# The first feed-forward batch prepared inside the last attention batch, in one program block

## The chip, the cores and the metric

The kernel runs on one core of one Trainium2 chip. The metric is the device time of one execution in microseconds (us); lower is better. A core has a matrix engine (TensorE, PE in the profile; its weight loads are listed as PEld), VectorE (DVE), ScalarE (ACT), GpSimd (POOL) and SyncE (SP), which here only issues DMAs. Each engine runs its own instructions in order, and they meet only at semaphores.

## The reference, cut to what matters

```python
x = L0_attn_x                                   # (8, 1024, 512)
mod = (_silu(L0_c) @ L0_wmod).reshape(8, 6, 1, 512)
sa, ca, ga, sb, cb, gb = mod[:, 0], ..., mod[:, 5]      # ga, gb: |gate| at least 0.25
h = _layernorm(x) * (1 + ca) + sa
x = x + ga * attn(h)         # 16 heads of 32; q, k, v = (h @ W + b) reshaped (b, h, dh, t);
                             # softmax over k.v * temperature, applied to q
h = _layernorm(x) * (1 + cb) + sb
x = x + gb * ffn(h)
# ffn: scores = h @ w_router; per batch the 512 of 1024 tokens with the highest scores are kept
#   processed = gelu(selected @ W1 + b1) @ W2 + b2       W1 (512, 2048), W2 (2048, 512)
#   output = hidden, plus sigmoid(score) * processed at the kept tokens
```

There are 8 batches of 1024 tokens.

## The kernel before, in words

There are two functions, each with its own SBUF and PSUM buffers and its own program block, one after the other: `attention_phase` and `ffn_phase`. At the end of a block all engines meet before the next one starts.

**Attention.** A loop over 8 batches holds 4 groups each, 32 groups in all. A group handles 256 tokens, as 16 pairs `p` of two units; a unit is one 128x1024 tile of scores. For a unit PE writes the scores into one of three PSUM slots (L408), DVE takes the row maximum (`row_max`, L702), ACT takes the exponential into `probs` (`exp_unit`, L595), which frees the slot, and PE multiplies the probabilities of an earlier pair with q (`products`, L455). Between these, PE makes k, v and q of the next group (L418, L430) and transposes its normalised rows (L441); ACT copies them out of PSUM (L568, L585, L575); POOL normalises, adds biases and splits values into two half-precision parts; DVE takes layernorm statistics (L660 of x, L745 of the new x) and divides q by the sums (L758, L763). POOL also finishes the group before: `residual` (L904), `normed_before`, `h_times`, `h_plus`, `base_times` and `base_plus` (L859 to L937), after which SP stores the rows `h_rows` and `out` (L344, L345); DVE makes the router scores (`dot_router`, L731). SP copies k and v into the stacks of the next group (L337).

**Rank.** Behind the loop SP writes the scores of all batches to memory, 4 bytes at a time (`store_scores`, L377), and loads those of batch 0 into every partition (`srow`, L382). For each of 8 tiles of tokens DVE counts the scores above (L77) and the equal ones that come earlier (L82), both over 1024 scores; `find_slots` turns the rank into a slot number (L90 to L97).

**Feed-forward.** All eight batches run the same body: a loop of 3 times two batches, then two batches written out. At the start SP loads W1 and W2 as eight pieces of 1 MB into four staging buffers (L1079); ACT makes the high part of each (`high_part`, L1157), DVE the low part (`low_part`, L1201). POOL stores number and weight of the kept tokens into `sel_rows` (`store_kept`, L104: 8 indirect DMAs); SP loads them as `kept` (L1064), DVE makes integers of them (`numbers`, L1206), POOL gathers rows of h into `hs` (L1276) and of the base into `bs` (L1279), PE transposes `hs` (L1106), and ACT and DVE make its two halves `fT` (L1162, L1211). Then for each of 16 slices `f`: `ff1` (12 matmuls, L1116), gelu on ACT (L1177), two splits on DVE (L1224, L1226) and `ff2` of the slice before (12 matmuls, L1129). Within the slices of one batch DVE also ranks the next one (one tile of tokens in each of slices 0 to 7, slots in slice 7, `numbers` in slice 10), and PE transposes its rows in slices 12 to 15. At the end DVE adds the bias (L1247), and POOL scales, adds the base and stores (L1294 to L1306).

## Time and profile before

| | us |
|---|---|
| median of 3 runs | 2504.0 |
| lowest and highest | 2500.78 and 2508.22 |
| profiled execution | 2516.56 |
| its span | 2514.8 |

| engine | busy us | share of the span |
|---|---|---|
| PE | 2284.4 | 91% |
| PEld | 899.7 | 36% |
| DVE | 1972.2 | 78% |
| ACT | 1483.7 | 59% |
| POOL | 1412.4 | 56% |

The span is the time between the first and the last record of the trace; 1.8 us lie around it. A busy share is a mean over stages: attention takes about two thirds of the span, the feed-forward part most of the rest, and each of them has to be read by itself, as does the stretch between them.

### The profile page before, as it was taken

Reading aid. Unit: us, or ns where it says so; the run is one execution under the profiler, and the core shown is the slowest. Engines: PE = TensorE matmul, PEld = TensorE weight load, DVE = VectorE, ACT = ScalarE, POOL = GpSimd, SP = SyncE. Lnnn points to the kernel's source line nnn. Section 1 sums busy time; section 2 is a strip of 40 time slices with the busy share of each in tenths; the row PEclk is TensorE's granted clock in tenths of the full one; section 3 lists DMA queues with packets and bytes.
Section 4 is the critical chain, followed back from the end, with each engine's and each line's share of the span. In section 5 each row is a group of like instructions: output and inputs, shape, how many; then the busy total and the mean of one; then the engine's idle time right before and its main releaser. Section 6 shows DMA issues by size and latency. Waiting matters only on the chain. (4 is left out here: it accounts for less than half of the span.)

```text
span 2514.8 us, 42424 instructions
## 1 busy us (share of the span) xinstructions
PE 2284.4 (91%) x12884; PEld 899.7 (36%) x12884; DVE 1972.2 (78%) x2698; ACT 1483.7 (59%) x2631; POOL 1412.4 (56%) x1233
## 2 busy tenths in 40 slices
PE   7999999999999999999999999950499999999996
PEld 2333333333333333333333333320244444444443
DVE  5899999999999999999999999953546645754632
ACT  1788888888888888888878888840311111111110
POOL 4566666676667666766666666660225444452531
PEclk9999999999999999999999999985699999999998
DMA  6233242333232333232233233373411112021110
GB/s 205 64 90 81 70 100 70 82 81 86 69 94 69 86 85 76 73 98 73 72 76 95 75 75 90 75 60 60 149 43 35 49 42 63 21 58 46 38 39 17
DMA packets 125227, 184.40 MB, mean 73 GB/s; under 512 B 43776, under 2 KB 43776, under 8 KB 124936
## 3 DMA queue, kind: packets, MB, share of 16 engines
q1 hardware_dynamic: 115216, 155.97, 25.9%
q0 software_dynamic: 9728, 25.23, 3.2%
q8 instruction: 108, 1.77, 0.3%
q14 instruction: 175, 1.43, 0.2%
HBM read 68.74 MB, written 43.16 MB: 44 GB/s over the span
## 5 line engine op out<-in xcount | busy, mean ns | idle before, releaser
L595 ACT ACTIVATE probs<-sc,nmax 128x1024 f32<-128x1024 f32 x1024 | 1137.2, 1116 | 249.7 <-DVE nmax L702 237.0
L702 DVE TENSOR_REDUCE nmax<-sc 128x1 f32<-128x1024 f32 x1024 | 1212.3, 1214 | 61.6 <-PE sc L408 55.8
L408 PE MATMUL sc<-stacks 128*128 128x512 f16 x2048 | 617.8, 383 | 51.8 <-ACT probs L595 36.5
L455 PE MATMUL acc<-probs,qn 128*32 128x512 f32 x4136 | 552.3, 606 | 2.1 <-DVE qn L763 1.2
L1177 ACT ACTIVATE g<-ff,b_col 128x512 f32<-128x512 f32 x128 | 88.0, 687 | 578.3 <-PE ff L1116 536.9
L1129 PE MATMUL ff<-w,g 128*128 128x512 f16 x1536 | 352.4, 379 | 14.7 <-DVE g L1226 13.9
L408 PEld LDWEIGHTS sc<-stacks 128*128 128x128 f16 x2048 | 154.6, 98 | 579.8 <-ACT probs L595 327.5
L1116 PE MATMUL ff<-fT,w 128*128 128x512 f16 x1536 | 353.9, 381 | 1.6 <-DVE fT L1211 1.6
L1224 DVE CAST g<-g 128x512 f16<-128x512 f32 x128 | 76.9, 600 | 290.8 <-ACT g L1177 243.5
L1129 PEld LDWEIGHTS ff<-w,g 128*128 128x128 f16 x1536 | 148.8, 98 | 199.2 <-DVE g L1226 21.5
L1116 PEld LDWEIGHTS ff<-fT,w 128*128 128x128 f16 x1536 | 151.0, 98 | 180.3 <-issue 5.7
L418 PE MATMUL pj<-wk,hT 128*128 128x512 f16 x792 | 205.8, 384 | 0.0
L595 ACT ACTIVATION_READ_ACCUMULATOR probs<-sc,nmax 128x1 f32 x1024 | 205.4, 201 | 0.0
L418 PE MATMUL pj<-wv,hT 128*128 128x512 f16 x792 | 202.6, 379 | 0.0
L430 PE MATMUL pj<-hT,wq 128*128 128x256 f16 x1584 | 194.2, 273 | 0.9 <-ACT qT L585 0.9
L430 PEld LDWEIGHTS pj<-hT,wq 128*128 128x128 f16 x1584 | 154.8, 98 | 46.5 <-ACT qT L585 1.2
L104 POOL DMA_INDIRECT sel_rows<-tok,slot x64 | 68.8, 1076 | 181.2 <-DVE slot L95 163.5
L913 POOL TENSOR_TENSOR hbuf<-hbuf,rows 128x1024 f32<-128x1024 f32 x66 | 155.8, 2361 | 17.8 <-DVE qn L763 17.6
L455 PEld LDWEIGHTS acc<-probs,qn 128*32 128x32 f32 x4136 | 81.6, 108 | 222.8 <-issue 217.2
L1294 POOL TENSOR_TENSOR y<-y,gb_row 128x512 f32<-128x512 f32 x32 | 46.6, 1461 | 192.0 <-DVE y L1247 192.0
L880 POOL TENSOR_TENSOR kv<-kv,k_bias 128x512 f32<-128x512 f32 x66 | 84.1, 1274 | 91.2 <-ACT kv L568 54.3
L880 POOL TENSOR_TENSOR kv<-kv,v_bias 128x512 f32<-128x512 f32 x66 | 84.5, 1281 | 87.0 <-ACT kv L568 87.0
(123 smaller groups left out, 2302.9 us busy)
## 6 DMA issues: line engine op xcount, KB each, us to landing
stacks<-k SPq DMA_DIRECT2D x528, 64.0 KB, 2.0
stacks<-v SPq DMA_DIRECT2D x528, 64.0 KB, 2.0
xt<-in_L_attn_x SPq DMA_DIRECT2D x140, 128.0 KB, 2.6
h_rows<-hbuf SPq DMA_DIRECT2D x132, 128.0 KB, 2.2
out<-base SPq DMA_DIRECT2D x132, 128.0 KB, 2.5
rows<-mod_rows SPq DMA_DIRECT2D x32, 256.0 KB, 4.0
stage<-in_L_ffn_W SPq DMA_DIRECT2D x8, 1024.0 KB, 9.9
probs<-in_L_wmod SPq DMA_DIRECT2D x4, 1024.0 KB, 10.7
```

The source lines that it names most:

```text
L408: mm = nc.tensor.matmul(slot(g, v)[:, half * D:(half + 1) * D], stacks[g % 2][:, 0, hq, i * P:(i + 1) * P], stacks[g % 2][:, 1, hq, half * ...
L418: mm = nc.tensor.matmul(pj[:], hT16[par][:, a, cc, p * P:(p + 1) * P], w[:, z, cc, :], start=(t == 0), stop=(t == len(terms) - 1))
L430: mm = nc.tensor.matmul(pj[:, ci * 2 * P:(ci + 1) * 2 * P], wq16[:, z, cc, co * P:(co + 1) * P], hT16[par][:, a, cc, :], start=(t == 0), s ...
L455: mm = nc.tensor.matmul(acc[at:at + DH, :], qn[:, (p // 2) % 2, p % 2, h2, :], probs[:, (2 * p + h2) % PROBS, half * D:(half + 1) * D], st ...
L595: nc.scalar.activation(probs[:, u % PROBS, :], slot(g, ring_at(p, h2)), ACT.Exp, bias=nmax[:, u % PROBS:u % PROBS + 1], accum_out=rsum[:, ...
L702: nc.vector.tensor_reduce(nmax[:, u % PROBS:u % PROBS + 1], slot(g, ring_at(p, h2)), AX.X, ALU.max, negate=True).then_inc(max_done, 1)
L880: nc.gpsimd.tensor_tensor(kv32[kk % 2][:], kv32[kk % 2][:], row, ALU.add).then_inc(kv_bias, 1)
L913: nc.gpsimd.tensor_tensor(dst, a, rows[:, row:row + 1, :].broadcast_to([P, SUBS, D]), op).then_inc(s_hm, 1)
L1116: mm = nc.tensor.matmul(ff[f % 2][:], w1_16[:, z, cc, f * P:(f + 1) * P], fT16[:, par, a, cc, :], start=(t == 0), stop=(t == len(terms) - 1))
L1129: mm = nc.tensor.matmul(acc[kt][:], g16[:, f % 2, a, kt * P:(kt + 1) * P], w2_16[:, z, f, :], start=(f == 0 and t == 0), stop=(f == FC - 1 ...
L1177: nc.scalar.activation(g32[:, f % 2, :], ff[f % 2][:], ACT.Gelu_apprx_tanh, bias=b1_col[:, f:f + 1], scale=1.0 / WS).then_inc(gelu_done, 1)
L1224: nc.vector.tensor_copy(g16[:, f % 2, 0, :], g32[:, f % 2, :]).then_inc(g_hi, 1)
```

## The change

Both phases become one function, `block_phases`, with one program block. Large buffers are shared: `room1` holds the attention weights and both `hT16`, and later W1; `room2` holds the even stacks, `k16`, `v16`, `hT32` and `kv32`, and later W2; `room3` holds `xhat` and three of the four `xt`, and later two staging buffers (four before). The feed-forward accumulators take the three PSUM slots, `acc` and `pj`.

- The attention loop runs 7 times, and the last batch is written out (`body(LAST, True)`). The feed-forward part has its first two batches written out, a loop of 2 times two, and two written out.
- `store_scores` moves into every attention batch, behind the row stores of group 1, for the batch before. `b1_col` (2048 biases, 4 bytes each) is loaded at the start of the kernel, ahead of the temperatures.
- `count_above` compares with "at least" for earlier tiles and "above" for the rest, together 1024 scores, and looks for equals over 128 only. `find_slots` has one more small addition.
- In the last batch DVE ranks batch 0 within groups 0 to 2 (`rank_first`), and POOL stores the kept numbers at the end of group 2 and gathers `hs` in group 3. The last group makes no k, v and q for a next one; the last two make no transposes, and the last three load no x and take no statistics of it. In group 3 SP loads weight pieces 0 to 2, ACT and DVE split pieces 0 (and ACT 1 and 2), and PE, ACT and DVE transpose and split the kept rows of batch 0.
- The other weight pieces (order W1, W2, W1, W2, ...) are loaded and split in slices of the first feed-forward batch (`first`), as are the statistics of the last group's x, its router scores, the scores and weights of batch 7 and the rank of batch 1, whose slots come in slice 8 and whose `numbers` come in slice 11.

```diff
-    nc.vector.tensor_scalar(r.cmp_out[:, 0], r.srow[:], r.s8[:, t:t + 1], 0.0, ALU.is_gt, ALU.add,
+    own = t * P
+        nc.vector.tensor_scalar(r.cmp_out[:, 0:own], r.srow[:, 0:own], r.s8[:, t:t + 1], 0.0, ALU.is_ge, ALU.add,
+                                accum_out=r.before[:, t:t + 1]).then_inc(r.s_cmp, 1)
+    nc.vector.tensor_scalar(r.cmp_out[:, own:T], r.srow[:, own:T], r.s8[:, t:t + 1], 0.0, ALU.is_gt, ALU.add,
...
# SP, attention body
+                    if last and g == 0:
+                        sp.wait_ge(s_sc, 16 * (B - 1))
+                        load_scores(0)
+                    if last and g == GB - 1:
+                        load_kept(0, 0)
+                        sp.wait_ge(t_pe, NG)
+                        load_weights(0)
                     sp.wait_ge(x2_done, b * GB + g + 1)
-                    load_x((g + 3) % 4, ahead[g])
-                    replicate((g + 1) % 2, 0, b * GB * 4 + 4 * (g + 1) + 2)
+                    if not (last and g >= GB - 3):
+                        load_x((g + 3) % 4, ahead[g])
+                    if last and g == GB - 1:
+                        load_weights(1)
+                        load_weights(2)
+                    else:
+                        replicate((g + 1) % 2, 0, b * GB * 4 + 4 * (g + 1) + 2)
...
+                    if g == 1:
+                        store_scores(batch_before)
...
# SP, behind the attention batches
+            load_weights(3)
+            sp.wait_ge(pv_done, ALL_PAIRS)
+            sp.dma_start(b2_row, b2.partition_broadcast(P)).then_inc(s_b, 16)
+            sp.wait_ge(r.s_slot, 1)
+            sp.wait_ge(s_sc, 16 * B)
+            load_scores(1)
+            sp.wait_ge(post_done, NG + 1)
+            store_rows(NG - 1, (NG - 1) % 2)
+            for j in range(4, 6):
+                load_weights(j)
+            sp.wait_ge(s_dot, 2 * NG + 2)
+            store_scores(B - 1)
+            for j in range(6, 8):
+                load_weights(j)
...
# ACT, last group, then the first feed-forward batch
+                        if end and p == 3:
...
+                            high_part(0)
+                        if end and p == 8:
+                            high_part(1)
+                        if end and p == 12:
+                            high_part(2)
+                        if end and p > NQ and p % 2 == 1:
+                            kept_high(0, 0, (p - NQ) // 2, aux[0])
...
+                    if first and f == 0:
+                        high_part(3)
+                    if first and f == 2:
+                        high_part(4)
+                    if first and f == 4:
+                        high_part(5)
...
# DVE, last batch, then the first feed-forward batch
+                if g == 0 and p == 7:
...
+                    count_above(nc, dve, r, 0, only)
+                if g == 0 and p == 14:
+                    count_above(nc, dve, r, 1, only)
...
+                if g == 2 and p == 8:
+                    dve.wait_ge(s_tok, 3)
+                    find_slots(nc, dve, r, r.tokens[:, 0:TB, :], only)
...
+                        if end and p == 1:
+                            numbers(0, 0)
+                        if end and p == 7:
+                            low_part(0)
+                        if end and p > NQ and p % 2 == 1:
+                            kept_low(0, 0, (p - NQ) // 2, aux[0])
...
+            q_over_sums(B, -1, PAIRS // 2 - 1)
+            low_part(1)
+            gated(B, -1, 1)
...
+                        if f == 0:
+                            low_part(2)
+                        if f == 1:
+                            for s in range(SUBS):
+                                stats_of_x2(B, 0, s)
+                            aggregate2(B, 0)
+                        if f == 2:
+                            low_part(3)
+                        if f == 3:
+                            count_tile(0)
+                            low_part(4)
...
+                        if f == 8:
+                            count_tile(6)
+                            count_tile(7)
+                            slots_of_next()
...
+                        if f == 11:
+                            numbers(nb, npar)
...
# POOL, last batch
+                    if last and g == GB - 2:
+                        wait_alone(r.s_slot, 1)
+                        store_kept(nc, r, sel_rows, range(0, TB // 2))
                     behind_qn(b, g, 7)
                     base_plus(b, g)
+                    if last and g == GB - 2:
+                        store_kept(nc, r, sel_rows, range(TB // 2, TB))
```

## Rows read from the trace of the kernel before

**Rows 1.** The page: busy tenths of PE in 40 slices of the span.

```profile
PE   7999999999999999999999999950499999999996
```

**Rows 2.** Windows by stage: length, then busy us (instructions) per engine, granted clock, DMA.

```profile
1568.50:1619.00 50.50, 49.35 (x307) 18.26 (x309) 48.68 (x64) 43.58 (x80) 34.25 (x30) 1.00 0.30 75
...
1672.50:1787.00 114.50, 0.00 (x0) 0.00 (x0) 38.54 (x62) 14.37 (x10) 37.08 (x27) 0.52 0.73 107
...
1805.90:1885.00 79.10, 79.10 (x376) 36.93 (x375) 39.07 (x72) 12.37 (x19) 15.47 (x16) 1.00 0.13 34
```

**Rows 3.** Timeline, the hand-over: start us, length us, engine, line, operation.

```profile
1668.61 1.12 ACT L595 ACTIVATE probs<-sc,nmax 128x1024 f32<-128x1024 f32 x1
...
1670.41 1.92 PE L455 MATMUL acc<-probs,qn 128*32 128x512 f32 x16 [1.21 <-DVE qn L763]
...
1674.30 11.50 SPq L377 DMA_DIRECT2D score_rows<-scores  x6
...
1676.99 0.25 DVE L750 BATCH_NORM_AGGREGATE mv<-stats 128x2 f32<-128x6 f32 x2 [0.15 <-DVE stats L745]
...
1687.82 2.34 POOL L937 TENSOR_TENSOR base<-base,x 128x1024 f32<-128x1024 f32 x1
1712.30 0.37 SPq L382 DMA_DIRECT2D srow<-score_rows  x1
```

**Rows 4.** Timeline, first weight pieces and first feed-forward matmuls.

```profile
1752.89 2.40 SPq L1079 DMA_DIRECT2D stage<-in_L_ffn_W  x4
...
1758.12 1.91 ACT L1157 ACTIVATE w<-stage 128x2048 f16<-128x2048 f32 x1 [3.33 <-DMA stage<-in_L_ffn_W]
...
1762.38 4.42 SPq L1079 DMA_DIRECT2D stage<-in_L_ffn_W  x1
...
1798.10 8.15 PE L1116 MATMUL ff<-fT,w 128*128 128x512 f16 x24 [1.60 <-DVE fT L1211]
```

**Rows 5.** Groups of instructions by shape, 1468 to 1670 us (four groups): busy us, mean ns.

```profile
L702 DVE TENSOR_REDUCE nmax<-sc 128x1 f32<-128x1024 f32 x129 | 152.8, 1215 | 6.5 <-PE sc L408 5.7 <-issue 0.2
...
L660 DVE BATCH_NORM_STATS2 stats<-xt 128x6 f32<-128x512 f32 x8 | 5.5, 682 | 0.0
...
L418 PE MATMUL pj<-wv,hT 128*128 128x512 f16 x96 | 24.6, 379 | 0.0
...
L430 PE MATMUL pj<-hT,wq 128*128 128x256 f16 x195 | 24.1, 273 | 0.0
```

**Rows 6.** Timeline, rank of the last batch up to the transposes of its rows.

```profile
2364.00 1.27 DVE L77 TENSOR_SCALAR_CACHE_REDUCE cmp_out<-srow,s 128x1024 bf16<-128x1024 f32 x1
...
2365.20 1.28 DVE L82 SCALAR_TENSOR_TENSOR cmp_out<-srow,s,earlier 128x1024 bf16<-128x1024 f32 x1
...
2367.01 0.22 DVE L95 SCALAR_TENSOR_TENSOR slot<-rank,first,drop 128x8 int32<-128x8 f32 x1
...
2377.16 0.98 POOL L104 DMA_INDIRECT sel_rows<-tok,slot  x1 [0.30 <-issue]
...
2381.24 0.17 DVE L1206 CAST kept_i<-kept 128x4 int32<-128x4 f32 x1 [1.12 <-DMA kept<-sel_rows]
...
2390.85 0.65 PE L1106 MATMUL aux<-id,hs 128*128 128x128 f32 x4 [0.25 <-DMA hs<-h_rows,kept_i]
```

**Rows 7.** Timeline, start of a feed-forward batch: a split beside POOL's work.

```profile
2338.00 1.48 DVE L1224 CAST g<-g 128x512 f16<-128x512 f32 x1
```

**Rows 8.** Waits of PE, 1798 to 2500 us: total us, times, longest.

```profile
PE ff L1129 <- DVE g L1226: 13.9, 13, 1.5
```

**Rows 9.** Timeline, start of the attention: two matmuls of scores at the low clock.

```profile
70.75 1.03 PE L408 MATMUL sc<-stacks 128*128 128x512 f16 x2 [2.20 <-DMA stacks<-v]
```

**Rows 10.** DMA issues by line: count, KB each, median us to landing.

```profile
score_rows<-scores SPq DMA_DIRECT2D x8, 4.0 KB, 21.1
...
b_col<-in_L_ffn_b SPq DMA_DIRECT2D x1, 8.0 KB, 10.7
```

**Rows 11.** Timeline of POOL in the group from 1568.5 us: `base_times`.

```profile
1613.12 2.80 POOL L913 TENSOR_TENSOR base<-hbuf,rows 128x1024 f32<-128x1024 f32 x1
```

More of the change, by code:

```diff
@@ L286, in attention_phase, with batches, n_of, only @@
         assert GB * RING % SLOTS == 0 and GB * UNITS % PROBS == 0
+        ALL_PAIRS = NG * PAIRS + LAG
+        ALL_FREED = SLOTS + NG * RING
+        LAST = B - 1
+        def batches(eng, body):
+            for par in range(2):
+                body(0, par, par == 0, False, False)
+            with eng.Fori(1, B // 2 - 1) as bb:
+                for par in range(2):
+                    body(bb, par, False, False, False)
+            for par in range(2):
+                body(B // 2 - 1, par, False, par == 1, True)
+        def n_of(bb, par, per, off):
+            return bb * (2 * per) + (per * par + off)
+        def only(per, off):
+            return off
         def mod_bank(j):
@@ L514, in _ @@
                     nxt = (g + 1) % 2
+                    end = last and g == GB - 1
                     for p in range(PAIRS):
@@ L546, in _ @@
                             whole(piece)
-                        if 2 * p + 2 == T_AT:
+                        if 2 * p + 2 == T_AT and not (last and g >= GB - 2):
                             pe.wait_ge(s_xhat, b * GB + g + 3)
@@ new lines, in low_part @@
+            def low_part(j):
+                k = j // 2
+                dve.wait_ge(w_hi, j + 1)
+                if j % 2 == 0:
+                    hi, lo = (w1_16[:, z, :, k * D:(k + 1) * D] for z in range(2))
+                else:
+                    hi, lo = (w2_16[:, z, 4 * k:4 * (k + 1), :] for z in range(2))
+                nc.vector.scalar_tensor_tensor(out=lo, in0=stage[:, j % 2], scalar=WS, in1=hi, op0=ALU.mult,
+                                               op1=ALU.subtract).then_inc(w_lo, 1)
@@ L773, in _, with body @@
+            def body(b, last):
                 for g in range(GB):
+                    load = not (last and g >= GB - 3)
+                    end = last and g == GB - 1
                     for p in range(PAIRS):
@@ L786, in _ @@
                             aggregate2(b, g)
[L787 removed]
+                        if (p == 9 or p == 11) and load:
                             if p == 9:
@@ L809, in _ @@
-            dve.wait_ge(r.s_const, 2)
-            nc.vector.tensor_copy(r.tokens[:, :, 0], r.tok_i[:]).then_inc(s_tok, 1)
-            nc.vector.memset(r.first[:], 0.0)
-            nc.vector.tensor_copy(r.s8[:], scores[:, 2:2 + TB])
-            weights(slice(0, (B - 1) * TB), 1)
-            dve.wait_ge(s_tok, 3)
-            dve.wait_ge(r.s_srow, 16)
-            for t in range(TB):
-                count_above(nc, dve, r, t, lambda per, off: off)
-            find_slots(nc, dve, r, r.tokens[:, 0:TB, :], lambda per, off: off)
@@ L825, in _ @@
+            batches(dve, ffn)
         @block.gpsimd
@@ L961, in _ @@
                     behind_qn(b, g, 4)
-                    split_kv(nxt, 2, n4 + 3)
+                    if not end:
+                        split_kv(nxt, 2, n4 + 3)
                     h_times(b, g)
```

740 lines of the change are left out of this document (389 added, 351 removed).

## The prediction, as it was made before the changed kernel ran

> **What bounds the kernel now.** I began with the busy slices of PE [rows 1]: PE is full in attention and in the feed-forward part, and two or three slices between them stand nearly empty. The windows [rows 2] put sizes to it. A group of attention lasts 50.5 us with PE busy 49.35 and DVE 48.68: both are full there, ACT (43.6) and POOL (34.3) are not. From 1672.5 to 1787 PE does nothing. So work moved into the last attention batch meets a full DVE; it isn't free because PE gets lighter.
>
> The hand-over, read in the timeline [rows 3, 4]: the last exponential ends at 1669.73 (call it E), PE's last products at 1672.33, and the first `ff1` starts at 1798.10. That is 125.8 us without useful matmuls. In order: seven score stores (1674.3 to 1712.3, 5.4 us each), sixteen counts and the slots (1716.7 to 1737), the last row stores and the meeting of the engines (to 1752.9), kept numbers, gather, weights, transposes (to 1798). Then the first 24 matmuls take 8.15 us, where later a matmul takes 0.216 (79.1 us for 376, transposes among them, [rows 2]) and 24 some 5.18.
>
> **The change, part by part.** Sum against the profiled execution, 2516.6 us; the median of the runs is 2504.0, 0.5% lower, and I apply the difference to it.
>
> *1. The gap.* `ff1` of batch 0 needs the split rows, the first weight piece and a free PSUM slot, all ready by E or soon after; PE's last products end at E + 2.6 and `ff1` can follow. Saved: **125.8 us**, less what follows.
>
> *2. DVE in the last batch.* A pass over 1024 scores starts 1.20 us after the one before (2364.00 to 2365.20, [rows 6]). With 0.13 us of it fixed (an estimate; the 8-element slot step is 0.22 long, same group) three passes over 1024 + 128 elements are 1.6 us, against 2.4 before. Eight tiles are 12.7; the slots 1.0, scores and weights 0.9, `numbers` 0.2, one `low_part` 2.2, four `kept_low` 2.4: 19.4. Gone are three groups' statistics of x, 6 x 0.68 [rows 5] and aggregation, 4.8. Net 14.6. In four groups DVE waits 6.5 us for PE [rows 5] and about 2 for others. If all of that slack takes up work, 6 us stay; if none, 14.6. PE is as full as DVE in groups 0 to 2, so a burst of DVE isn't made good later there; in group 3 PE loses 12.3 of k and v and 6 of q (half of 24.6, a quarter of 24.1, [rows 5]) and DVE is the only bound. I take **+10.5**.
>
> *3. ACT in the last group.* It loses k, v, q and transposed copies and gains three `high_part` of 1.91 [rows 4] and four copies of 0.6, some 45 us of work in 52. But each 1.91 delays a slot, and the three slots give DVE about 1 us of room (estimated from its spacing of 1.5 us per unit): 3 x 1. **+3** (0 to 6).
>
> *4. A new wait in group 3.* DVE does `numbers` behind pair 1 of group 3, and the rest of its row maxima is queued behind it, so all engines wait with it. POOL reaches `base_times` 44.6 us into a group [rows 11], here about 3 earlier since it splits no hT and 2 later with the longer group: 43.5. Then 2.4, four indirect stores of 1.29, `base_plus` 2.4, four more stores: 58.7; from there `numbers` came 3.1 us behind the last store's end (2378.14 to 2381.24, [rows 6]): 62. DVE gets there at 52.5 + 6.8 = 59.3. **+3** (0 to 8). POOL's gather (4 x 1.27) ends ahead of its `residual`. SP's first weight piece, queued behind the kept numbers, needs 5.2 us from issue to ACT (1752.89 to 1758.12, [rows 4]) and comes to ACT at pair 3 just in time.
>
> *5. The start.* The b1 load of 2048 single elements now stands ahead of the temperatures, Wq and further modulation weights, while the DMA engines are full. The nearest rows: it landed after 10.7 us [rows 10], SP's next load then took 4.4 us to issue (at 1762.38, [rows 4]), and a store of 1024 such elements took 5.4. **+4** (0 to 10). The same kind of store in each attention batch comes at the start of group 2, some 20 us before the next copies of k: nothing, unless it takes longer than it did. The Trainium skill (DMA: Bandwidth & Descriptors, Specifications) puts the least transfer for full rate at 512 bytes; the rate of 4 KB in 5.4 us agrees, and a reader may leave the page out.
>
> *6. The first feed-forward batch.* Here a chain speaks against the change. S = E + 2.6 is the start of `ff1` 0, a slice's 12 matmuls are 2.59 us. ACT's `high_part(3)` behind gelu 0 waits for a piece that SP may load only after `low_part(1)` (S + 0.4): landed S + 6, done S + 8, gelu 1 done S + 8.7, its split S + 9.9, then the statistics of the last group: S + 11.5. Only now can POOL normalise that group: statistics to `base_plus` took 12.9 us (1677.24 to 1690.16, [rows 3]), S + 24.4. SP waits for just that, issues 8 row stores (4 us), then weight piece 4: S + 28.9, landed about 8 us later among 2 MB of other transfers (5.2 to 10): S + 37. ACT stands at `high_part(4)` behind gelu 2 since S + 11.3, with gelu 3 queued behind it. So split 3 ends at S + 40.9, and PE, done with `ff1` 4 at S + 20.7, waits for it: **+20.2** (14 to 25). In such a wait PE's clock falls: after the hand-over 24 matmuls took 8.15 for 5.18 [rows 4] and the granted clock of the empty stretch was 0.52 [rows 2], near the lower of its two levels, 1.2 GHz: **+3**.
> The second wait: the slots of batch 1 come in slice 8, not 7. By DVE's queue from S + 40.9 (counts, low parts, router scores between splits) they are ready at S + 70.6. From slots to landed rows took 23.6 us (2367.2 to 2390.8, [rows 6]): S + 94.2. PE reaches the transposes behind `ff2` 11 at S + 87.7: **+6.5** (3 to 10). Behind 94.2 come four transposes of 0.44, three `ff1` and four `ff2`, 19.9: it ends at S + 114.1. Before, the first batch took 87.4 (1798.1 to 1885.5; PE full to 1885, [rows 2]). Difference **+26.7**, the 3 us of clock being in both.
>
> *7. The other seven batches.* At their start DVE's splits run beside POOL's work and take 1.48 us for 0.43 [rows 7], and PE waits for them 13.9 us in all [rows 8], some 2.2 in each of six batches that also count. Counts 0.8 shorter let the second and third split end earlier: about 1.4 a batch, **-8** (-11 to 0).
>
> Sum: -125.8 + 10.5 + 3 + 3 + 4 + 26.7 - 8 = **-86.6**; 2516.6 becomes 2430, and on the median 2504 - 87 = **2417 us**.
>
> **The rivals.**
> *A, the covers hold.* DVE's slack takes the rank, `numbers` doesn't wait, weight piece 4 lands at S + 34 and the transposes wait 3: 6 + 1 + 0 + 1 + 20 - 10 on -125.8 is -108: 2396. For it: DVE has 8 us of waits in four groups. Against: the wait for piece 4 is in the program's order and doesn't hang on a price.
> *B, the inserts cost their full time.* 14.6 + 6 + 7 + 8 + 33 - 3 = +65.6 on -125.8 is -60: 2444. For it: PE and DVE take turns with three slots, and a burst on one is felt by the other.
> *C, PE goes to its low clock in group 3*, since it is busy only 32 of 52 us there. At 1.2 GHz two score matmuls take 1.03 [rows 9] for 0.61, eight products twice 1.06: 32 x 1.03 + 16 x 2.1 + 4 is 70, and the group lasts 15 to 18 us longer: 2433. Against: its gaps would be about a microsecond, and with such gaps in attention the granted clock was 1.00 [rows 2]. The Trainium skill (TensorE: Matmul & The Clock Gate, Part 1: The HAM clock gate) has half rate as the state of an idle engine that activity lifts; by it C is possible, and the clock after the empty stretch agrees (0.52).
> *D, slower than before.* The score stores within the loop hold up the copies of k and v in the DMA queues. The place is SP's queue at the start of group 2; the next copies come 22 us into the group. The gain of 87 is spent when each of seven batches loses 12.4 us, so from some 34 us per store on. It took 5.4 in a row of seven [rows 3], though a landing of 21.1 us stands as the median, queued behind each other [rows 10]. At 36 us per store: 2519.
> *E, the hand-over isn't emptied.* The chain slots, stores, kept numbers, gather isn't done when the transposes of group 3 are due, and a serial stretch returns. It would have to slip by some 20 us before PE waits; were it late by 105, 2500.
>
> **How the numbers follow.** Forecast 2417, its own range 2405 to 2430 (parts 4 to 7 within half their bounds): 0.50. A 0.20, B 0.20, C 0.05, D 0.02, E 0.03. A range of 2388 to 2450 takes in the forecast, C and nearly all of A and B and leaves out D, E and the tails, under 2 in 10. 0.3% is 7.5 us, about what this measurement can tell from no change: faster 0.95 (forecast, A, B, C), same 0.03 (E), slower 0.02 (D).
>
> **What would show it.** Part 1: no PE gap over some 5 us between the last products and `ff1`. Parts 2 to 4: the last batch takes 218 us instead of 202, with a DVE wait at `numbers` of about 3. Part 5: the first scores at 75 instead of 70.8. Part 6: ACT waits for stage piece 4 for some 25 us in slice 2, PE some 20 behind `ff1` 4, then some 6 for the gathered rows. Part 7: six batches of about 86 us instead of 87.5. I would be wrong if PE runs through slices 2 to 4 without a gap, if the loop's groups leave 50.5 us, or if group 3 shows a clock under 0.9.

## The result and the profile after

| | before | after |
|---|---|---|
| median, us | 2504.06 | 2433.23 |
| lowest and highest of 4 runs | 2500.78 and 2508.22 | 2431.43 and 2438.28 |
| profiled execution | 2516.56 | 2431.43 |
| its span | 2514.8 | 2429.7 |

The ratio of the times is 0.9715, with a 95% interval from 0.9704 to 0.9727: 71 us faster. The forecast was 2417, 87 us faster, with a range of 2388 to 2450.

The page of the changed kernel: busy tenths of PE and its granted clock, in 40 slices of the span.

```profile
PE   7999999999999999999999999877689999999996
PEclk9999999999999999999999999999899999999998
```

The slices 5, 0 and 4 of [rows 1] are gone. In their place stand five dented ones: the last attention batch (8, 7, 7) and the first feed-forward batch (6, 8).

The end of attention in the timeline of the changed kernel (start us, length us, engine, line, operation): last exponential, last products, first `ff1`.

```profile
1687.88 1.11 ACT L804 ACTIVATE probs<-sc,nmax 128x1024 f32<-128x1024 f32 x1
...
1689.68 1.92 PE L599 MATMUL acc<-probs,qn 128*32 128x512 f32 x16 [2.33 <-DVE qn L1037]
...
1691.53 0.39 PE L728 MATMUL sc<-qT,room 128*128 128x512 f16 x1
```

`ff1` begins as the last products end. The 125.8 us of [rows 3, 4] have become nothing.

What was given back shows in the waits of all engines of the changed kernel, 1680 to 1850 us (total us, times, longest).

```profile
ACT room L825 <- DMA room<-in_L_ffn_W: 32.9, 3, 28.4
...
PE sc L741 <- DVE probs L1165: 22.5, 1, 22.5
...
PE pj L659 <- DMA stacks<-h_rows,kept_i: 8.6, 1, 8.6
```

And in SP's own queue, changed kernel: row stores of the last group, then weight pieces 4 and 5.

```profile
1718.35 0.34 SPq L436 DMA_DIRECT2D h_rows<-hbuf  x1
...
1721.80 0.43 SPq L437 DMA_DIRECT2D out<-base  x1
1722.27 1.38 SPq L472 DMA_DIRECT2D room<-in_L_ffn_W  x2
```

SP issues piece 4 at 1722.27, right behind the eight stores. ScalarE stood for it until 1731.2, the splits behind it came late, and PE stood 22.5 us. That is the chain of step 6 of the forecast.

For the last attention batch I cut both traces at the start of the last exponential of each group. Columns: length, then busy us (instructions) of PE, PEld, DVE, ACT and POOL, granted clock, DMA share, GB/s. First a further profiled execution of the kernel before (2503.05 us, near its median), then the changed kernel.

```profile
1465.20:1516.30 51.10, 49.45 (x306) 17.95 (x306) 47.54 (x65) 42.46 (x77) 32.89 (x29) 1.00 0.32 80
1516.30:1565.30 49.00, 48.03 (x300) 17.71 (x296) 47.30 (x65) 42.09 (x78) 32.87 (x29) 1.00 0.36 94
...
1614.40:1663.60 49.20, 48.22 (x306) 17.76 (x302) 47.31 (x64) 42.12 (x78) 32.90 (x29) 1.00 0.31 77
```

```profile
1461.30:1514.50 53.20, 49.27 (x302) 17.58 (x298) 51.52 (x76) 42.31 (x77) 32.87 (x29) 1.00 0.37 91
1514.50:1571.40 56.90, 49.98 (x297) 16.84 (x296) 55.10 (x85) 42.18 (x79) 32.44 (x29) 1.00 0.31 75
1571.40:1627.10 55.70, 48.88 (x283) 16.42 (x286) 51.89 (x75) 40.93 (x74) 29.39 (x26) 0.97 0.21 47
1627.10:1687.90 60.80, 41.40 (x222) 9.10 (x214) 50.37 (x64) 44.23 (x73) 26.06 (x19) 0.92 0.30 89
```

In group 1 DVE is 7.8 us busier (55.10 for 47.30) and the group 7.9 us longer, with DVE 97% busy both times: no slack took up work there. Group 0 did hide some (4.0 us more work, 2.1 us more time), group 2 (before: DVE busy 47.30 of 49.10) the reverse (4.6 and 6.6). Together the three have 16.4 us more work and take 16.6 us longer. Group 3 is 11.6 us longer though DVE has only 3 us more to do: there something waits.

How far can one group of one trace be trusted? Group 1 has the same code in the changed kernel and in nine of those built on it below. It lasts 56.9 us in six of these ten and 58.1 or 58.2 in four. Group 2 has the same code in nine and lasts 54.0 to 57.9. So a difference of a microsecond in group 1, or of one to four in group 2, needs no cause in an edit. Group 3, with all its inserts and the wait in place, stays within 60.8 to 61.6 in the changed kernel and in the four below that leave it as it is.

Where the time went, stage by stage, against both profiled executions of the kernel before. The stages are cut at the starts of the last exponential of an attention batch, of the first `ff1` and of the writes of y.

| stage | before, 2516.56 | before, 2503.05 | after | difference to each |
|---|---|---|---|---|
| start and seven attention batches | 1469.5 | 1465.2 | 1461.3 | -8.2, -3.9 |
| last attention batch | 199.1 | 198.4 | 226.6 | +27.5, +28.2 |
| last exponential to first `ff1` | 129.5 | 122.9 | 3.6 | -125.9, -119.3 |
| first feed-forward batch | 87.6 | 86.2 | 121.1 | +33.4, +34.8 |
| other batches, to the last y | 609.1 | 608.6 | 597.2 | -11.9, -11.4 |
| to the end of the span | 19.9 | 19.9 | 19.9 | 0, 0 |
| sum | 2514.8 | 2501.3 | 2429.7 | -85.1, -71.6 |

The profiled execution that the forecast was made on was 12.5 us above its median, and 6.6 us of that lay in the hand-over, which the change takes out whole. Against it the change looks worth 85 us; against a typical one, 72. The difference in the first line is not shown to be the change's. Start and seven batches take 1463.4 to 1469.5 us in three traces of the old program (the third has only the cheaper count, below) and 1461.3 to 1465.1 in eleven of the new one, and these ranges overlap.

### The profile page after: what moved, and what is told of

It reads as the page before. It is cut to its first block, busy times and chain, and to the rows that moved or that the text cites. A ratio compares the mean times of both kernels' runs of the same rounds, so it can differ in the third digit from the quotient of the medians.

```text
span 2429.7 us, 41301 instructions
## 1 busy us (share of the span) xinstructions
PE 2272.0 (94%) x12772; PEld 886.5 (36%) x12772; DVE 1903.2 (78%) x2806; ACT 1477.5 (61%) x2616; POOL 1367.7 (56%) x1205
## 4 chain that ended last, share of the span: by engine, by line
PE 65%; DVE 16%; issue 9%; POOL 4%; ACT 3%; DMA 1%; SPq 1%; DVEq 0%; POOLq 0%; ACTq 0%
PE sc L552 13%; PE sc L741 13%; PE acc L599 13%; PE sc L728 12%; DVE nmax L976 9%; PE pj L562 8%; PE pj L574 5%; POOL x L1314 3%; DVE qn L1037 2%; ACT probs L804 2%; DVE stats L1019 1%; PE sc L585 1%; PE sc L614 1%; DVE rinv L1032 0%; DMA room<-in_L_ffn_W 0%
## 5 line engine op out<-in xcount | busy, mean ns | idle before, releaser
L562 PE MATMUL pj<-room 128*128 128x512 f16 x1536 | 395.3, 381 | 0.4 <-ACT qT L794 0.4
L741 PE MATMUL sc<-room,probs 128*128 128x512 f16 x1536 | 354.7, 381 | 26.8 <-DVE probs L1165 26.8
L552 PE MATMUL sc<-room 128*128 128x512 f16 x1024 | 309.4, 384 | 40.7 <-ACT probs L804 24.1
L552 PE MATMUL sc<-stacks 128*128 128x512 f16 x1024 | 309.6, 384 | 38.3 <-ACT probs L804 37.7
L741 PEld LDWEIGHTS sc<-room,probs 128*128 128x128 f16 x1536 | 150.3, 98 | 209.8 <-DVE probs L1165 27.6
L562 PEld LDWEIGHTS pj<-room 128*128 128x128 f16 x1536 | 150.1, 98 | 188.4 <-issue 8.9
L574 PE MATMUL pj<-room 128*128 128x256 f16 x1536 | 188.3, 273 | 1.1 <-ACT qT L794 0.9
L728 PE MATMUL sc<-stacks,room 128*128 128x512 f16 x768 | 175.6, 379 | 0.0
L574 PEld LDWEIGHTS pj<-room 128*128 128x128 f16 x1536 | 150.0, 98 | 45.5 <-ACT qT L794 1.8
L728 PE MATMUL sc<-qT,room 128*128 128x512 f16 x512 | 163.4, 382 | 1.1 <-issue 1.1
L1294 POOL TENSOR_TENSOR room<-room 128x512 f16<-128x512 f32 x128 | 149.0, 1164 | 10.6
```

What stands on the lines that cost most here:

```text
L552: mm = nc.tensor.matmul(slot(g, v)[:, half * D:(half + 1) * D], stacks[g % 2][:, 0, hq, i * P:(i + 1) * P], stacks[g % 2][:, 1, hq, half * ...
L562: mm = nc.tensor.matmul(pj[:], hT16[par][:, a, cc, p * P:(p + 1) * P], w[:, z, cc, :], start=(t == 0), stop=(t == len(terms) - 1))
L574: mm = nc.tensor.matmul(pj[:, ci * 2 * P:(ci + 1) * 2 * P], wq16[:, z, cc, co * P:(co + 1) * P], hT16[par][:, a, cc, :], start=(t == 0), s ...
L728: mm = nc.tensor.matmul(ff[f % 2], w1_16[:, z, cc, f * P:(f + 1) * P], fT16[par][a][:, cc, :], start=(t == 0), stop=(t == len(terms) - 1))
L741: mm = nc.tensor.matmul(ff2[kt], g16[:, f % 2, a, kt * P:(kt + 1) * P], w2_16[:, z, f, :], start=(f == 0 and t == 0), stop=(f == FC - 1 an ...
L1294: nc.gpsimd.tensor_tensor(dst[:, 1], kv32[kk % 2][:], dst[:, 0], ALU.subtract).then_inc(kv_split, 1)
```

## The experiments

The theory at this point: PE's wait for weight piece 4 and the late gathered rows are two waits in series in the first feed-forward batch; in the last attention batch DVE's added work counts in full; group 3 has a further loss in SP's chain. The rival for each: some other engine or DMA traffic holds the same time, so that the wait moves and doesn't go.

A ratio is to runs of the kernel before taken beside each experiment, whose medians lie between 2504.8 and 2509.1 us. So differences between two kernels are better read from the ratios (0.001 is 2.5 us) than from the times.

**The kernel before, once more.** It gave the second column of the table.

> The kernel before, profiled once more, to see what of the 85 us between the two profiled executions belongs to the change. Theory 1 (the profiled execution of before was a long one, 12.5 us above its median, and the surplus lies in the start and in the attention loop): the empty stretch of PE between last products and first ff1 is again 125 to 127 us, and the first scores start earlier than 70.8 us or the loop's seventh batch is reached earlier than 1400.9 us. Theory 2 (the surplus lies in the hand-over itself, in the 4-byte stores): the empty stretch is 113 to 118 us, and start and loop are as in the first profile.

Measured: 2503.05 us. From last products to first `ff1` 119.2 us, with 4.8 us for each store of the scores where [rows 3] has 5.4.

**Weight pieces 4 and 5 ahead of the last row stores.**

```diff
+            for j in range(4, 6):
+                load_weights(j)
             sp.wait_ge(post_done, NG + 1)
             store_rows(NG - 1, (NG - 1) % 2)
-            for j in range(4, 6):
-                load_weights(j)
```

> The changed kernel with SP's loads of weight pieces 4 and 5 ahead of its wait for the last base_plus and of the last row stores. Theory: the wait of ACT for piece 4 (28.4 us) and PE's wait of 22.5 us behind it go away, and so does the low clock behind it (about 2.6 us); the wait for gathered rows (8.6 us) stays within 2 us. 24 to 26 us faster than the changed kernel, some 2408 us. Rival (the empty time is only handed on: the piece still lands late among row stores and gather, or another wait, for the router scores or the base, takes its place): 0 to 12 us faster, with a PE wait of over 10 us elsewhere in the first feed-forward batch.

Measured: 2419.17 us, ratio to the kernel before 0.9647 (0.963 to 0.9665): 14 us less than the changed kernel by the times and 17 by the ratios, not 24 to 26. The waits of PE in this kernel, 1690 to 1800 us:

```profile
PE pj L659 <- DMA stacks<-h_rows,kept_i: 9.4, 1, 9.4
PE sc L741 <- DVE probs L1165: 3.5, 2, 2.8
```

The wait for piece 4 is gone but for 3.5 us, so its cause is shown. From first `ff1` to first y it takes 103.2 us for 121.1: 17.8 us less in the stage that was changed. In attention, which was not, this profiled execution is 5.2 us longer. The second wait stayed, and part of the gain went to DVE, whose splits now run beside POOL's work for the last group (timeline of DVE, same kernel):

```profile
1714.91 2.20 DVE L1163 CAST probs<-probs 128x512 f16<-128x512 f32 x1 [1.83 <-ACT probs L878]
1717.15 2.72 DVE L1165 TENSOR_TENSOR probs<-probs 128x512 f16<-128x512 f32 x1
1719.79 2.32 DVE L1153 COPY s<-scores 128x8 f32<-128x8 f32 x1
```

With POOL idle these take 0.43, 0.69 and 0.17 us (the copy in the changed kernel, at 1734.81). In the changed kernel most of this work of POOL fell into the time in which DVE stood still anyway. The Trainium skill (GPSIMD Engine Reference, Specifications) says that GpSimd's SBUF interfaces are shared with VectorE, with contention for some kinds of VectorE instructions. That these three are slow beside POOL and fast without it agrees.

**The biases loaded last at the start.** The load of `b1_col` moves behind all other first loads.

```diff
-                sp.dma_start(b1_col[:], b1.rearrange("(f p) -> p f", p=P)).then_inc(s_b, 16)
...
             load_x(2, 2)
+            with nc.allow_non_contiguous_dma(reason="2048 biases, once"):
+                sp.dma_start(b1_col[:], b1.rearrange("(f p) -> p f", p=P)).then_inc(s_b, 16)
```

> The changed kernel with the load of b1 (2048 single elements) behind the last loads of the start, not ahead of the temperatures. Prediction's part 5: 4 us faster (0 to 10), the first scores start 3 to 5 us earlier than 67.0 us. Rival (the start isn't held by that load, as the profile of after suggests with first scores at 67.0 against 70.8): within 1 us of the changed kernel.

Measured: 2434.23 us, ratio 0.9707 (0.9691 to 0.9724): not to be told from the changed kernel, though the intervals leave room for some 3 us. The first scores start at 68.5 us here, 67.0 in the changed kernel, 68.8 and 70.8 in the two of before. With the load moved they come later and not earlier, so it does not hold up the start.

**The rank of batch 0 done twice**, with the second results unused.

```diff
                     count_above(nc, dve, r, 0, only)
+                    again(0)
```

> The changed kernel with each of the eight counts of batch 0 in the last attention batch done twice (23 more passes on DVE, 12.7 us of work, plus their waits). Theory (DVE bounds the last attention batch and its slack is used up): 11 to 15 us slower than the changed kernel. Rival (a good part is covered by waits of DVE for PE and ACT): 4 to 9 us slower. If it is over 16, the inserts cost more than their length, by disturbing the turn of PE, DVE and ACT.

Measured: 2451.35 us, ratio 0.9774 (0.9755 to 0.9792): 18 us above the changed kernel by the times, 15 by the ratios, for 12.7 us of added passes. The groups of the last attention batch:

```profile
1464.40:1522.30 57.90, 50.42 (x302) 18.72 (x298) 54.93 (x86) 42.60 (x77) 32.88 (x29) 0.96 0.38 90
1522.30:1586.80 64.50, 53.53 (x298) 18.17 (x296) 60.94 (x109) 42.28 (x79) 32.49 (x29) 0.93 0.28 67
```

The columns are those of the windows above. The groups are 4.7 and 7.6 us longer than in the changed kernel, 14.7 in all four. DVE is busy 12.7 us more in them. So work on DVE costs here about its length, or a little more. In the two groups above PE's clock is lower, 0.96 and 0.93 where the changed kernel has 1.00; whether that is the surplus was not shown.

**The slots of batch 1 in slice 7** (built on the kernel with pieces 4 and 5 early): DVE's list of the first feed-forward batch is put in another order.

```diff
+                            count_tile(0)
                         if f == 2:
...
-                        if f == 8:
+                        if f == 6:
+                            low_part(4)
                             count_tile(6)
+                        if f == 7:
                             count_tile(7)
                             slots_of_next()
+                            low_part(5)
+                        if f == 8:
+                            weights(slice(LAST * TB, B * TB), 2)
```

> The kernel with weight pieces 4 and 5 loaded early (e1), and in the first feed-forward batch VectorE ranks batch 1 earlier: tile 0 behind the statistics in slice 1, tiles 1 and 2 in slice 3, 3 in slice 4, 4 and 5 in slice 5, 6 in slice 6, 7 and the slots in slice 7; low parts 4, 5 move to slices 6 and 7. My theory: the 9.4 us that PE waits for the gathered rows in e1 is the chain slots, stores, kept numbers, gather (20 us from slots at 1752.2 to landed rows), so 6 us earlier slots take 6 to 9 us off: 2410 to 2413 against 2419. Rival: the DMA side (weight pieces 6 and 7, 4-byte numbers) sets when the rows land, and the wait moves by less than 2 us: 2418 to 2421. Second rival: counts beside POOL's work in slice 3 cost three times their length and delay the splits that PE waits for, giving the gain back: 2417 to 2422.

Measured: 2408.42 us, ratio 0.9611 (0.9595 to 0.9627): 11 us less than without it by the times, 9 by the ratios. The waits of PE, 1690 to 1800 us:

```profile
PE sc L741 <- DVE probs L1165: 5.2, 3, 4.3
PE pj L659 <- DMA stacks<-h_rows,kept_i: 2.9, 1, 2.9
```

The wait for the gathered rows fell from 9.4 to 2.9 us, so it was the chain from DVE's rank. The wait for DVE's splits grew from 3.5 to 5.2: a small part of what the second rival said. From first `ff1` to first y it takes 96.9 us for 103.2. That is what the new order gave, 6.4 us, the 4.8 of the two waits and some clock: without the new order PE ran at 0.50 for six microseconds behind the longer wait. Nearly all the rest of the gain in these two traces (5.4 us) lies ahead of the first `ff1`, where nothing was changed.

**POOL's stores of the kept numbers earlier in group 2.**

```diff
+                    if last and g == GB - 2:
+                        wait_alone(r.s_slot, 1)
+                        store_kept(nc, r, sel_rows, range(0, TB // 2))
                     behind_qn(b, g, 6)
...
                     base_times(b, g)
                     if last and g == GB - 2:
-                        wait_alone(r.s_slot, 1)
-                        store_kept(nc, r, sel_rows, range(0, TB // 2))
+                        store_kept(nc, r, sel_rows, range(TB // 2, TB))
                     behind_qn(b, g, 7)
                     base_plus(b, g)
-                    if last and g == GB - 2:
-                        store_kept(nc, r, sel_rows, range(TB // 2, TB))
```

The first four stores stand one step earlier, behind the last split of v.

> e4, and in group 2 of the last attention batch POOL stores the kept numbers ahead of its work on the base rows instead of around it (first four behind the last split of v, four behind the product with the gate). My theory: the wait of VectorE at the integer kept numbers in group 3 (4.5 us in the changed kernel) goes, and the whole group with it: 4 us less than e4. Rival: VectorE's wait only stands in for one that comes anyway (ScalarE and PE have their own work to catch up with, or POOL's late rows delay the next group), and the time stays within 1.5 us of e4.

Measured: 2412.16 us, ratio 0.9632 (0.9606 to 0.9659): no gain. SP's queue shows why:

```profile
1637.62 0.33 SPq L436 DMA_DIRECT2D h_rows<-hbuf  x1
...
1642.01 0.43 SPq L437 DMA_DIRECT2D out<-base  x1
1642.48 0.43 SPq L461 DMA_DIRECT2D kept<-sel_rows  x1
```

SP loads the kept numbers only behind the row stores of group 2, and those wait for `base_plus`, which now came behind all eight stores of POOL. DVE waited 5.2 us at `numbers` instead of 4.5. I had moved the work on POOL and left out the queue of SP between it and DVE.

**The inserts of group 3 made tiny** (changed kernel).

```diff
-                            high_part(0)
+                            high_part(0, True)
...
-                            low_part(0)
+                            low_part(0, True)
...
+                if few:
+                    dst, src = dst[:, 0:1, 0:2], src[:, 0:1, 0:2]
```

> The changed kernel, in which the high parts of weight pieces 0, 1 and 2 and the low part of piece 0 take 2 columns in the last attention group instead of 2048 (so most of W1's first piece, the high half of W2's first and W1's second piece are left out, and the output with them); waits and loads stay. It measures what these four inserts cost group 3: 3 x 1.9 us on ScalarE, 2.3 us on VectorE. My forecast had +3 for ScalarE's and 2.2 of VectorE's time: about 5 us less than the changed kernel, 2428. Rival (the inserts cost their full length and push PE to its low clock): 8 to 14 us less, 2419 to 2425, and the granted clock of the group's second half above 0.9 where it was 0.65 to 0.91. Second rival: nothing, VectorE's other work bounds the group.

Measured: 2431.12 us, ratio 0.9698 (0.9682 to 0.9714), 2 us less than the changed kernel by the times, 4 by the ratios, and not clearly to be told from it. Its last group lasted 56.3 us for 60.8, 4.5 less:

```profile
1516.40:1574.60 58.20, 51.44 (x297) 16.93 (x296) 55.22 (x85) 42.30 (x79) 32.45 (x29) 0.97 0.31 75
1574.60:1631.20 56.60, 51.28 (x283) 16.76 (x286) 51.99 (x75) 40.84 (x74) 29.17 (x26) 0.91 0.21 46
1631.20:1687.50 56.30, 41.45 (x222) 9.24 (x214) 48.06 (x64) 39.63 (x73) 24.25 (x19) 0.91 0.34 97
```

But groups 1 and 2, in which nothing was changed, lasted 2.2 us longer, with a clock of 0.97 and 0.91. That is within the spread of these groups. The 4.5 us of group 3 are not, so the four inserts cost about that, near the 5.2 of steps 2 and 3 together. The wait at `numbers` stands in this group too, 4.9 us long.

**Only the cheaper count**, in the kernel before: two blocks and the hand-over stay as they were.

```diff
-    nc.vector.tensor_scalar(r.cmp_out[:, 0], r.srow[:], r.s8[:, t:t + 1], 0.0, ALU.is_gt, ALU.add,
...
+        nc.vector.tensor_scalar(r.cmp_out[:, 0, 0:own], r.srow[:, 0:own], r.s8[:, t:t + 1], 0.0, ALU.is_ge, ALU.add,
+                                accum_out=r.before[:, t:t + 1]).then_inc(r.s_cmp, 1)
+    nc.vector.tensor_scalar(r.cmp_out[:, 0, own:T], r.srow[:, own:T], r.s8[:, t:t + 1], 0.0, ALU.is_gt, ALU.add,
...
```

> The kernel before (two program blocks, rank between them) with only the new count_above and find_slots: 1152 scores per tile in three passes instead of 2048 in two. My theory: seven feed-forward batches that rank the next one become about 2 us shorter each, as in the changed kernel (85.5 for 87.5), and the rank in the hand-over by 8 x 0.8 = 6 us: 2504 - 20 = 2484 (2482 to 2490). Rival from my forecast: 1.4 us per batch, so 2504 - 10 - 6 = 2488. Second rival: the shorter batches come from something else in the new program (PSUM places, buffers), and only the 6 us of the hand-over show: 2498.

Measured: 2484.33 us, ratio 0.9919 (0.99 to 0.9938): 20 us faster, as the first theory said. The writes of y in this kernel, and PE's waits from 1866 us on:

```profile
1866.46 2.48 DVE L1258 SCALAR_TENSOR_TENSOR y<-ff,b_row 128x512 f32<-128x512 f32 x4 [1.27 <-PE ff L1140]
1951.96 2.48 DVE L1258 SCALAR_TENSOR_TENSOR y<-ff,b_row 128x512 f32<-128x512 f32 x4 [1.27 <-PE ff L1140]
```

```profile
PE ff L1140 <- DVE g L1237: 5.0, 7, 0.8
```

A batch takes 85.5 us, as in the changed kernel, for 87.5 before, and PE's waits for splits are 5.0 us for 13.9 [rows 8]. So the small edit in `count_above` alone is worth 20 us in the old program. From the first to the last y it saves 11.8 us (596.8 for 608.6), nearly all of the 11.9 or 11.4 that these batches gained in the changed kernel; most of the rest lies in the hand-over.

**`numbers` behind pair 3, and the high parts late.** Three kernels on top of the one with the slots in slice 7: the integer kept numbers behind pair 3 instead of 1; high parts of pieces 1 and 2 behind the last exponential and gelu 0; both.

```diff
-                        if end and p == 1:
+                        if end and p == 3:
                             numbers(0, 0)
```

```diff
-                        if end and p == 8:
-                            high_part(1)
-                        if end and p == 12:
-                            high_part(2)
...
+            high_part(1)
             act.wait_ge(s_d, 1)
...
                     if first and f == 0:
+                        high_part(2)
+                    if first and f == 1:
                         high_part(3)
```

> e4 (weight pieces 4 and 5 early, slots of batch 1 in slice 7), and VectorE makes the integer kept numbers behind pair 3 of the last attention group instead of pair 1. The kept numbers land in the box's row order at 1639.7 us of e4, where VectorE stands since 1635.2; POOL's gather starts only behind the division of pair 4, at 1643.6. My theory: the wait of 4.5 us goes from the group and nothing takes its place, since VectorE bounds it: 2408 becomes 2403 to 2405, group 3 lasts 56 to 57 us for 60.8. Rival (as in e5, which gained nothing): the group is held by ScalarE's inserts and three slots, and the time stays at 2407 to 2410. Second rival: the gather comes later and PE waits for the rows at pair 8 of the group: slower than e4 by 2 to 5 us.

> e4, and ScalarE makes the high parts of weight pieces 1 and 2 behind the last exponential and behind gelu 0 instead of within the last attention group (high part 3 follows behind gelu 1). If ScalarE's inserts delay VectorE by the slots they hold back, as the shrunk inserts showed (group 3 lasted 56.3 us for 60.8 with all four inserts gone), two of them moved out give back 2 to 3 us in the group, and cost nothing behind it, where ScalarE waits for PE: 2405 to 2406. Rival: half of that saving was VectorE's low part alone, and the moved parts delay the low parts of pieces 1 and 2 and with them PE in slice 1 or 4: 2408 to 2411.

> Both changes of the two runs beside it. If both theories hold they add up: 4.5 + 2.5 us under e4, 2400 to 2403, since one is a wait of VectorE early in the group and the other a wait for slots in its middle. If one of them fails, the time is that of the other alone; if the wait at the numbers had covered part of what ScalarE catches up with, the sum is smaller than the parts by about 2 us.

Measured: 2412.58 us, ratio 0.9627 (0.961 to 0.9644); 2409.13 us, ratio 0.9618 (0.9598 to 0.9638); 2409.58 us, ratio 0.9614 (0.9596 to 0.9631). None can be told from the kernel they build on (0.9611), so the 2403 to 2405 of the first, the 2405 to 2406 of the second and the 2400 to 2403 of both together did not come. With the high parts late the last group did shrink, to 57.4 us for 60.8, with a wait at `numbers` of 4.8 still in it:

```profile
1630.60:1688.00 57.40, 40.17 (x213) 8.48 (x212) 49.02 (x64) 41.03 (x70) 25.08 (x19) 0.91 0.32 93
```

With `numbers` at pair 3 alone it didn't shrink (60.4). The kernel with both shows what took the place of the wait, first DVE's wait in its last group, then ScalarE's:

```profile
DVE rinv L1031 <- ACT probs L804: 3.8, 1, 3.8
```

```profile
ACT room L825 <- DMA room<-in_L_ffn_W: 3.6, 1, 3.6
```

DVE no longer waits for the kept numbers, but ScalarE now stands at the high part of piece 0, and DVE behind it. SP issues that piece behind the kept numbers, for which it waits until POOL's last store has landed. The wait at `numbers` had covered this one.

**Piece 0 ahead of the kept numbers**, on top of both.

```diff
-                        load_kept(0, 0)
                         sp.wait_ge(t_pe, NG)
                         load_weights(0)
+                        load_kept(0, 0)
```

> The kernel with both changes of the run before (kept numbers made behind pair 3, high parts of pieces 1 and 2 late), and SP loads weight piece 0 ahead of the kept numbers instead of behind them. There the wait at the numbers was gone but ScalarE stood 3.6 us at the high part of piece 0 in pair 3, because SP issues that load only behind the kept numbers, for which it waits 4.7 us until POOL's last store has landed; VectorE then stood 3.8 us for ScalarE. My theory: these two waits are one chain in SP's queue, and without it group 3 lasts about 54 us for 57.9: ratio to the kernel before 0.9600 (0.959 to 0.961) for 0.9614, that is 2404 to 2407 where the kernel before takes 2504 to 2507. Rival: a third wait takes their place (PE at its low clock, or the kept numbers landing later behind the megabyte of weights, so that VectorE stands at pair 3 again): group 3 stays at 57 to 58 us and the ratio at 0.961 to 0.963.

Measured: 2402.91 us (2399.93 to 2406.73), ratio 0.9592 (0.9577 to 0.9607). This is the lowest ratio of all and as expected (0.959 to 0.961), but its interval overlaps that of its base. ScalarE's and DVE's waits in the last group are now small. First ScalarE, then DVE:

```profile
ACT room L825 <- DMA room<-in_L_ffn_W: 1.1, 1, 1.1
```

```profile
DVE kept_i L1067 <- DMA kept<-sel_rows: 0.7, 1, 0.7
...
DVE rinv L1031 <- ACT probs L804: 0.5, 1, 0.5
```

So these two waits did come from SP's order. But the theory also said that group 3 would last 54 us, and its rival that it would stay at 57 to 58. Groups 2 and 3, first of the kernel with both changes, then of this one:

```profile
1575.50:1632.20 56.70, 49.94 (x289) 16.57 (x288) 52.34 (x75) 40.86 (x73) 30.48 (x26) 0.97 0.22 48
1632.20:1690.10 57.90, 40.56 (x212) 9.16 (x212) 49.06 (x64) 41.12 (x70) 25.07 (x19) 0.88 0.31 92
```

```profile
1572.30:1626.30 54.00, 48.50 (x283) 16.57 (x286) 51.85 (x75) 40.73 (x73) 29.09 (x26) 0.97 0.22 48
1626.30:1683.90 57.60, 42.38 (x222) 9.11 (x214) 50.54 (x64) 41.20 (x70) 26.40 (x19) 0.88 0.33 95
```

Group 3 went from 57.9 to 57.6 us, as the rival said. DVE waits less there, but the same 64 instructions keep it busy 1.5 us longer. The 2.7 us of group 2 lie where nothing was edited, within the spread of that group. The gain of this kernel over its base is therefore not shown to come from the new order, and the expected ratio was met partly by luck.

## Why the prediction was right or wrong, step by step

The sign, the mechanism and the range held. The time was 16 us above the forecast. The sum on the profiled execution (2430) met the measured 2431.4, but partly by luck, with errors that cancel. Against that execution the last attention batch cost 11 us more than the parts 2 to 4 had it (27.5 for 16.5) and the first feed-forward batch 6.7 more. The start and seven batches came out 12.2 us under the expected +4, and the other batches 3.9 us under theirs.

**1, the gap: right, but carried to the wrong base.** -125.8 expected, -125.9 measured against the same execution. The step that failed is "I apply the difference to it" for the median. A stage of DMA waits that is removed whole takes its own run-to-run excess with it: this stage took 122.9 us in an execution near the median, 129.5 in the profiled one. With the difference to the start and the loop (4.3) this makes up most of the 12.5 us between that execution and the median, which are the larger part of the 16 by which the forecast missed.

**2, DVE in the last batch: mis-sized.** Two things were off. Of a net 14.6 us of added work I let 4.1 vanish in DVE's waits, and over groups 0 to 2 none did: 16.4 us more work, 16.6 us more time (2.1, 7.9 and 6.6; the execution near the median as base), and the doubled rank cost about its length. The slack I had read in the window of 50.5 us was not there in groups cut at their own ends (49.0, DVE 47.3). And the work itself was 19.4 us over the four groups: three of the eight tie passes, beside POOL's work, took 1.42 us for 0.35. The terms of rival B for this batch add up to the 27.6 us that it cost, but not one by one: it had the four inserts of group 3 at full length, over 8 us, and they cost about 4.5.

**3, ScalarE's inserts: right in size.** With `low_part(0)`, of step 2, they cost 4.5 us, where I had 3 + 2.2.

**4, the wait at `numbers`: there, but its price is not shown.** 3 us expected, 4.5 measured as a wait of DVE. With the high parts late, group 3 lasts 57.4 us with a wait of 4.8 in it. With both edits and the weight piece first it lasts 57.6 with one of 0.7. So taking the wait away gave nothing back. That weight piece 0 would come "just in time" held only because DVE stood at `numbers` before it; with `numbers` moved, ScalarE waited for it. In all, group 3 grew by 11.6 us. The four inserts are 4.5 of that; the other 7.1 stay open. PE's low clock is in there, in part: 0.92 over the group, 0.65 from 1666 to 1674 us, behind waits of up to 4.2 us. Rival C was right that it falls, and wrong in its price: the group lasted 60.8 us and not 70. That its total, 2433, is the measured median is chance.

**5, the start: wrong.** +4 expected. The moved load of `b1_col` showed no cost at the start. The 3.9 to 8.2 us by which the start and seven batches were shorter are not clear of what this part differs by between executions, so no gain is shown either.

**6, the first feed-forward batch: right in its links, a little short.** Piece 4: 22.5 us for 20.2. Gathered rows: 8.6 for 6.5. The difference of the batch: +33.4 for +26.7. The clock was 0.51 in the 5 us behind the first wait and 0.92 over the 21 us behind the second, so it fell twice and not once. That there are two separate causes was shown by taking away one after the other: in this batch 17.8 us, then 6.4.

**7, the other batches: right, mis-sized.** -2.0 us each and -11.9 in all for -8. The cheaper count alone gave the same 85.5 us per batch.

**The other rivals and marks.** A fell with steps 2, 4 and 6: too little of it was covered. D and E did not come: stores within the loop left its groups at 49.2 us, as before, and the transposes of batch 0 found their rows. The 50.5 us that I had named as the length of a loop's group was a window wider than a group; the same misreading is in the 44.6 us at which step 4 has POOL reach `base_times`, some 1.8 too many.

## What to carry to other kernels

When a dead stretch is emptied, look at what its emptiness was hiding: here a gate in one in-order queue (row stores ahead of a weight load) cost 22.5 us that no engine's busy time showed, and two lines in another order gave 17.8 us of the batch back. Removing a wait is not yet removing time. Moving `numbers` alone only uncovered the next customer of the same queue, and with both waits gone the group still lasted as long. And set a forecast on the stage times of more than one execution, cut at the period of the loop, above all where the stage that goes is made of DMA waits. Do the same before a difference of a few microseconds in one stage is given to an edit.

## What was unexpected of the hardware

- Two executions of one kernel differed by 13.5 us (2516.56 and 2503.05), 6.6 of it in one stretch of small stores: 5.4 or 4.8 us for each store of 4 KB in 4-byte elements.
- A DVE pass beside POOL's work can take far more than the 1.48 for 0.43 us of [rows 7]: 2.20 for 0.43, 2.72 for 0.69, 2.32 for 0.17 (a copy of 8 columns), 1.42 for 0.35.
- PE's clock fell within attention, towards the lower of its two levels: 0.65 in 1666 to 1674 us of the changed kernel, behind a wait of 3.4 us, with PE busy 16.0 of the 25 us before. With the rank doubled it was 0.93 over a whole group.

```profile
1641.00:1666.00 25.00, 15.96 (x80) 3.18 (x80) 22.14 (x29) 20.22 (x33) 13.28 (x11) 0.91 0.41 135
1666.00:1674.00 8.00, 8.00 (x38) 2.19 (x36) 6.20 (x8) 4.95 (x9) 2.37 (x1) 0.65 0.00 0
```

- The same short wait lowered the clock in one execution and not in another. At the end of group 0 PE waits 1.74 us in the changed kernel and 1.75 with the biases last, in the same code. The clock stayed at 1.00 in the first and fell to 0.50 from 1518 to 1520 us in the second; the group behind it lasted 56.9 and 58.2 us.
- Switching ScalarE from gelu to the exponential and back in the first feed-forward batch took two table loads of 1.28 us. The Trainium skill (ScalarE: Activation LUTs, What ACT_TABLE_LOAD costs) has 1283 ns for one, and the trace agrees. The drain of about 1380 ns that it adds to each does not show: in the changed kernel a load starts 0.02 us behind the end of the gelu, and the next exponential 0.01 us behind the load.
